# State-space stage of a decoder kernel: other slots for ScalarE's reads, another order of two pieces on TensorE, two decays per unit in SBUF

## The reference, cut to what matters

```python
def _mamba(x, Win, convw, convb, Wx, Wdt, bdt, Alog, Dp, Wout):
    xi, z = jnp.split(x @ Win, 2, axis=-1)               # 256 channels each
    xi = silu(_causal_dwconv(xi, convw, convb))          # 4 taps
    dt_in, Bm, Cm = split(xi @ Wx)                       # 8, 16, 16
    dt = softplus(dt_in @ Wdt + bdt);  A = -exp(Alog)    # A: 256 x 16
    # per channel and state s: h_t = exp(dt_t*A) * h_(t-1) + dt_t*u_t*B_t ;  y_t = sum_s h_t*C_t
    y = _selective_scan(xi, dt, A, Bm, Cm, Dp)           # + u*Dp
    return y * silu(z) @ Wout
# forward and backward, each + x and normed, summed, then relu(. @ W1 + b1) @ W2 + b2, + sum, normed
```

## Time and profile before

| | us |
|---|---|
| median of 3 runs | 5266.18 (5259.53 to 5272.27) |
| the profiled execution | 5254.81 |
| its span in the trace | 5252.9 |
| state-space stage, first scan at 71.0, last at | 2473.7 |
| busy over the span: PE, DVE, ACT, POOL | 4029.3, 4122.6, 2797.7, 2811.0 |
| one scan, one product by C on DVE (mean) | 1.217, 0.661 |
| one decay on ACT, one input on POOL (mean) | 0.688, 1.323 |

### The profile page before, as it was taken

The page is one execution under the profiler, slowest core; times in us unless marked ns, Lnnn a source line. Parts: engine busy times, 40 slices in busy tenths (PEclk is TensorE's granted clock), DMA queues, the critical chain, the costliest instruction groups (busy, mean ns, idle before and its releaser), DMA issues. The chain is left out here.

```text
span 5252.9 us, 104514 instructions
## 1 busy us (share of the span) xinstructions
PE 4029.3 (77%) x29689; PEld 2335.5 (44%) x29692; DVE 4122.6 (78%) x8425; ACT 2797.7 (53%) x6477; POOL 2811.0 (54%) x3454
## 2 busy tenths in 40 slices
PE   5788787878878877877688868886283888789953
PEld 2333333333333333332466646665282666566632
DVE  5998888899888889987588877776145887767778
ACT  4555555555555555554577744444374554444435
POOL 5766666666666666765477742333543222233345
PEclk8988888898888888988799979996695999889965
DMA  2111110111111111100455535555114554365521
GB/s 87 69 39 67 71 71 37 71 71 67 38 71 71 39 69 71 71 35 39 94 108 105 105 78 118 113 116 159 51 53 119 108 108 99 75 129 116 111 56 32
DMA packets 320704, 420.70 MB, mean 80 GB/s; under 512 B 40512, under 2 KB 302224, under 8 KB 309648
## 3 DMA queue, kind: packets, MB, share of 16 engines
q1 hardware_dynamic: 316048, 408.35, 29.9%
q0 software_dynamic: 4352, 8.95, 0.5%
HBM read 307.65 MB, written 109.58 MB: 79 GB/s over the span
## 5 line engine op out<-in xcount | busy, mean ns | idle before, releaser
L1861 PE MATMUL bank<-m_h,ident 128*128 128x512 f32 x2048 | 1241.8, 701 | 423.8 <-DVE m_h L2127 371.7
L2228 POOL TENSOR_TENSOR m_h<-m_dtu,m_Bb 128x512 f32<-128x512 f32 x1024 | 1327.0, 1323 | 336.5 <-PE bank L1861 331.0
L2121 DVE TENSOR_TENSOR_SCAN m_h<-bank,m_h 128x512 f32<-128x512 f32 x1024 | 1246.3, 1217 | 192.8 <-ACT bank L2009 183.8
L2009 ACT ACTIVATE bank<-m_dt,m_A 128x512 f32<-128x512 f32 x1024 | 695.4, 688 | 748.0 <-DVE m_h L2121 662.0
L1861 PEld LDWEIGHTS bank<-m_h,ident 128*128 128x128 f32 x2048 | 390.7, 214 | 1081.4 <-DVE m_h L2127 847.1
L2127 DVE TENSOR_TENSOR m_h<-m_h,bank 128x512 f32<-128x512 f32 x1024 | 676.8, 661 | 6.7 <-PE bank L1854 6.7
L712 DVE TENSOR_REDUCE x_nm<-bank 128x4 f32<-128x308 f32 x512 | 239.3, 474 | 149.9 <-PE bank L370 144.3
L547 ACT ACTIVATE x_sm<-bank,x_nm 128x77 f32<-128x77 f32 x1024 | 318.2, 336 | 60.3 <-DVE x_nm L712 59.9
L537 ACT ACTIVATE f_pT<-bank 128x512 f32<-128x512 f32 x256 | 153.0, 598 | 239.9 <-PE bank L390 238.6
L1805 PE MATMUL bank<-m_xTp,m_wck 128*128 128x512 f32 x512 | 268.7, 630 | 12.1 <-ACT m_xTp L1923 12.1
L537 ACT ACTIVATE a_pT<-bank 128x512 f32<-128x512 f32 x256 | 153.4, 599 | 181.3 <-PE bank L390 180.3
(11 more groups left out here) (425 smaller groups left out, 9876.4 us busy)
## 6 DMA issues: line engine op xcount, KB each, us to landing
m_Bb<-m_B SPq DMA_DIRECT2D x32, 4096.0 KB, 12.2
x_Ks<-x_k_parts SPq DMA_DIRECT2D x64, 231.0 KB
x_q_parts<-x_qp SPq DMA_DIRECT2D x32, 384.0 KB, 3.9
x_Qs<-x_q_parts SPq DMA_DIRECT2D x32, 384.0 KB
f_Ks<-f_k_parts SPq DMA_DIRECT2D x32, 384.0 KB
a_Ks<-a_k_parts SPq DMA_DIRECT2D x32, 384.0 KB
x_xp<-x_stage SPq DMA_DIRECT2D x32, 256.0 KB
x_Qs<-x_q_parts SPq DMA_DIRECT2D x32, 256.0 KB
```

Of the source, the lines that this page charges most:

```text
L1861: pe.matmul(banks[4 + c], ident[:], h[:, k % RING, :], start=(s == 0), stop=(s == NS - 1)).then_inc(s_ya.sem, 1)
L2009: act.activation(decays[k % AHEAD], dt[:, d, c, :], ACT.Exp, scale=A[:, d, c, s:s + 1]).then_inc(s_dA.sem, 1)
L2121: v.tensor_tensor_scan(h[:, k % RING, :], decays[k % AHEAD], h[:, k % RING, :], 0.0, ALU.mult, ALU.add).then_inc(s_h.sem, 1)
L2228: pool.tensor_tensor(h[:, k % RING, :], dtu[:, d, c, :], Bb[:, d, s, :], ALU.mult).then_inc(s_dB.sem, 1)
```

## The change

The two extra decay buffers are in SBUF (`spare_decays`); `decay_buffer` picks them for slots 26 and 27 of d=0 and 25 and 26 of d=1. `last_reader` gives the scan that last read a buffer, in place of the fixed k-2: for a decay in SBUF it lies in the unit before, and for the next decays in the banks four slots back. `exp` is parted into `exp` and `one`. In `PE_AT` of d=1 `xT` comes ahead of `f:0`; `yT`, `m0`, `m1` and (in d=1) `dt0`, `dt1` move one to three slots back. In `ACT_AT` the reads of `f`, `c1`, `dt0`, `yT`, `m0`, `m1`, `o` move back by up to five slots, `dt1` of d=0 moves two slots forward, `log` and `move` move back; in `DVE_AT` `f_stats`, `f_affine`, `e`, `o_stats`, `dtu` of d=1 follow. `POOL_AT` stays.

```diff
--- before.py
+++ after.py
@@ -1541,7 +1541,6 @@
     SL = NS * NC
     RING = 8
     LAG = 2
-    AHEAD = 2
     TURNS = NG // 2
     PADS = CK - 1
     BROW, CROW, XM = 32, 64, 96
@@ -1592,19 +1591,22 @@
 
 
     PE_AT = ({0: ["xT"], 1: ["c0:0"], 2: ["c0:1", "o:0", "c0:2"], 7: ["o:1", "c0:3"], 8: ["o:2"], 10: ["z0"], 11:
-              ["c1:0", "c1:1", "c1:2", "c1:3"], 14: ["z1", "xd:0", "xd:1"], 17: ["dt0"], 18: ["dt1"], 21: ["yT:0"],
-              22: ["yT:1"], 24: ["m0"], 27: ["m1"]},
-             {0: ["f:0", "xT"], 1: ["f:1", "c1:0"], 2: ["c0:0"], 3: ["c1:1", "c1:2"], 6: ["c0:1"], 7: ["c1:3"], 8:
-              ["c0:2"], 9: ["c0:3"], 12: ["z0"], 14: ["z1", "xd:0", "xd:1"], 16: ["dt0"], 17: ["dt1"], 21: ["o:0"],
+              ["c1:0", "c1:1", "c1:2", "c1:3"], 14: ["z1", "xd:0", "xd:1"], 17: ["dt0"], 18: ["dt1"], 22: ["yT:0"],
+              23: ["yT:1"], 27: ["m0"], 28: ["m1"]},
+             {0: ["xT", "f:0"], 1: ["f:1", "c1:0"], 2: ["c0:0"], 3: ["c1:1", "c1:2"], 6: ["c0:1"], 7: ["c1:3"], 8:
+              ["c0:2"], 9: ["c0:3"], 12: ["z0"], 14: ["z1", "xd:0", "xd:1"], 17: ["dt0"], 18: ["dt1"], 21: ["o:0"],
               23: ["o:1", "o:2"]})
-    ACT_AT = ({0: ["xT"], 10: ["c0"], 11: ["o"], 12: ["z0"], 14: ["o_norm", "c1"], 16: ["z1"], 17: ["xd"], 19: ["dt0"], 23: ["dt1", "exp", "yT"], 25: ["log"], 26: ["move"], 27: ["m1"], 29: ["m0"]},
-              {0: ["xT"], 1: ["f"], 6: ["f_norm"], 10: ["c1"], 12: ["c0"], 13: ["f_out"], 14: ["z0"], 16: ["z1", "xd"], 20: ["dt0"], 21: ["dt1"], 22: ["exp"], 24: ["log", "o"], 26: ["move"], 29: ["o_norm"]})
+    ACT_AT = ({0: ["xT"], 10: ["c0"], 11: ["o"], 12: ["z0"], 14: ["o_norm", "c1"], 16: ["z1"], 17: ["xd"], 20: ["dt0"],
+               21: ["dt1"], 22: ["exp"], 23: ["one"], 27: ["log"], 28: ["yT"], 29: ["move"], 30: ["m0"], 31: ["m1"]},
+              {0: ["xT"], 4: ["f"], 9: ["f_norm"], 11: ["c1"], 12: ["c0"], 14: ["z0"], 15: ["f_out"], 16: ["z1"], 17: ["xd"],
+               20: ["dt0"], 21: ["dt1"], 22: ["exp"], 23: ["one"], 26: ["log"], 27: ["o"], 28: ["move"], 31: ["o_norm"]})
     DVE_AT = ({0: ["y"], 11: ["o_stats"], 14: ["z0", "u"], 15: ["z0_read"], 17: ["z1"], 18: ["z1_read"], 22: ["rest"], 23:
                ["e"], 29: ["lo"], 30: ["dtu"]},
-              {2: ["y", "f_stats"], 8: ["f_affine"], 13: ["u", "z0"], 14: ["z0_read"], 15: ["z1"], 16: ["z1_read"], 21: ["rest"],
-               22: ["e"], 25: ["o_stats"], 28: ["dtu"], 29: ["lo"]})
+              {2: ["y"], 5: ["f_stats"], 10: ["f_affine"], 13: ["u", "z0"], 14: ["z0_read"], 15: ["z1"], 16: ["z1_read"],
+               21: ["rest"], 23: ["e"], 27: ["o_stats"], 29: ["lo"], 30: ["dtu"]})
     POOL_AT = ({4: ["gated"], 15: ["o_pow"], 31: ["dt", "far"]},
                {8: ["f_pow"], 13: ["out_pow"], 14: ["gated"], 26: ["dt"], 30: ["o_pow"], 31: ["far"]})
+    IN_SBUF = ((26, 27), (25, 26))
     LAST = ("y", "gated", "o", "o_stats", "o_pow", "o_norm")
 
     def side(at, g, d, k):
@@ -1612,7 +1614,7 @@
         for what in at[d].get(k, []):
             name = what.split(":")[0]
             kind = name if name in PREP else ("o" if name in LAST else ("f" if name[0] == "f" and name != "far" else name))
-            if kind in ("u", "z0_read", "z1_read", "move", "exp", "log", "rest", "lo", "e", "dtu", "dt", "far"):
+            if kind in ("u", "z0_read", "z1_read", "move", "exp", "one", "log", "rest", "lo", "e", "dtu", "dt", "far"):
                 kind = "xT"
             if kind == "out_pow":
                 kind = "f"
@@ -1692,7 +1694,19 @@
         x_g, o_g = [t.rearrange("(g b) t d -> g t b d", b=GB) for t in (x, y)]
         turned_by = (ident, flip)
         convw = Bb[:, 0, 0:4, :].rearrange("p a t -> p (a t)")
-        decays = (banks[0], banks[1])
+        spare = sb("spare_decays", [P, 2, GT])
+
+        def decay_buffer(d, k):
+
+            return spare[:, k % 2, :] if k in IN_SBUF[d] else banks[k % 2]
+
+        def last_reader(d, k):
+
+            back = 2
+            while ((k - back) % SL in IN_SBUF[(d + (k - back) // SL) % 2]) != (k in IN_SBUF[d]):
+                back += 2
+            return k - back
+
         block = st.enter_context(nc.Block())
 
         def schedule(turn):
@@ -1958,6 +1972,7 @@
                 if what == "exp":
                     act.wait_ge(s_ab.sem, s_ab.at(n + 1))
                     act.activation(flat(cc[:]), flat(cc[:]), ACT.Exp, scale=-1.0).then_inc(s_z.sem, 1)
+                if what == "one":
                     act.wait_ge(s_z.sem, s_z.at(n + 1))
                     act.activation(flat(tu[:]), flat(cc[:]), ACT.Identity, bias=one[:]).then_inc(s_w1.sem, 1)
                 if what == "log":
@@ -2005,8 +2020,8 @@
                 s, c = k // NC, k % NC
                 if k == 0:
                     act.wait_ge(s_dt.sem, s_dt.at(n + 1))
-                act.wait_ge(s_h.sem, s_h.at(n, k + 1 - AHEAD))
-                act.activation(decays[k % AHEAD], dt[:, d, c, :], ACT.Exp, scale=A[:, d, c, s:s + 1]).then_inc(s_dA.sem, 1)
+                act.wait_ge(s_h.sem, s_h.at(n, last_reader(d, k) + 1))
+                act.activation(decay_buffer(d, k), dt[:, d, c, :], ACT.Exp, scale=A[:, d, c, s:s + 1]).then_inc(s_dA.sem, 1)
 
             def work(at, what, g, l, d):
 
@@ -2029,7 +2044,7 @@
                 for l in range(2):
                     for d in range(2):
                         unit(2 * i + l, l, d)
-            for what in ("xT", "c1", "c0", "z0", "z1", "xd", "move", "dt0", "dt1", "exp", "log"):
+            for what in ("xT", "c1", "c0", "z0", "z1", "xd", "move", "dt0", "dt1", "exp", "one", "log"):
                 prep(use_first, 0, 0, what)
             schedule(turn)(act)
             for d, names in ((0, ("o", "o_norm", "yT", "m0", "m1")), (1, ("f", "f_norm", "f_out"))):
@@ -2118,7 +2133,7 @@
             def scan(v, n, d, k):
                 v.wait_ge(s_dA.sem, s_dA.at(n, k + 1))
                 v.wait_ge(s_dB.sem, s_dB.at(n, k + 1))
-                v.tensor_tensor_scan(h[:, k % RING, :], decays[k % AHEAD], h[:, k % RING, :], 0.0, ALU.mult, ALU.add).then_inc(s_h.sem, 1)
+                v.tensor_tensor_scan(h[:, k % RING, :], decay_buffer(d, k), h[:, k % RING, :], 0.0, ALU.mult, ALU.add).then_inc(s_h.sem, 1)
 
             def times_C(v, n, k):
                 s = k // NC
```

## The result

The changed kernel takes 5185.08 us (median of 4 runs, 5177.53 to 5197.9) against 5262.85 for the kernel before (4 runs, 5259.41 to 5272.27): a ratio of 0.9852, 95% interval 0.9827 to 0.9877, so 65 to 91 us less. Forecast were 5201, in a range of 5122 to 5240.

What follows compares the result with a forecast made beforehand. DVE, busy 2170.64 of the state-space stage's 2406.00 us, was taken as the bound. Gross gain 165 less 98 and 2 gives 65 us: the profiled 5254.81 becomes 5190, the median 5201; range 5122 to 5240.

Steps and rivals of the forecast that it cites:

- waits for ScalarE: Scans' waits for decays at slots 24 to 28 go; 32 us stay at slot 1 of d=1: 152 us gained.
- `lo`: In d=1, every second unit, it meets GpSimd idle instead of mid-inputs: 0.7 us, where it took 1.75; 10 us gained.
- waits for the spread C: Products on DVE waiting for TensorE's spread C, 6.7 us: half of it goes, 3 us gained.
- scans 25, 26 and input 27 of d=1: SBUF-decay scans meet GpSimd's two `dt` operations, making input 27 late for scan 27: 4.4 us a unit lost.
- scans 26, 27 of d=0: SBUF-decay scans meet GpSimd's input 31 and first `dt`: between 0.7 and 2.7 us, taken as 2.0 a unit lost.
- input 0 of the next unit: `dtu` one to two slots later in d=1 leaves GpSimd's input 0 just in time: 16 x 0.1 = 2 us lost.
- The lock: DVE operations with both inputs in SBUF wait for a running GpSimd operation; two scans a unit now do: 98 us with input 27.
- no lock: Rival: SBUF-decay scans are not held by GpSimd, only input 27 is late; 130 us gained, 5136 us; chance 0.20.
- GpSimd keeps the ports for its whole queue: Rival: waiting scans in slots 25 to 28 are not let in between GpSimd operations; 90 us slower, 5356 us; chance 0.06.
- input 27 is tied to `e`: In d=1, fixed durations from `e` through logarithm and `dt` make input 27 late for scan 27: 2.2 us without port conflicts.
- part 3: TensorE's `xT` ahead of `f:0` at the start of d=1 shortens scan 1's wait: 1.34 us, 1.6 at half clock.
- part 1: Side results read later on ScalarE: the slot 28 wait of d=0 (3.78 us) and the 5 us pile-up before decay 24 go.

Runs made afterwards that it cites:

- Experiment 1: Changed kernel with all decays back in the two PSUM banks, none in SBUF; 5176.79 us, ratio 0.9862.
- experiment 2: Changed kernel with one SBUF decay a unit, at slot 30 where GpSimd is idle, instead of two; 5180.45 us, ratio 0.9844.
- experiment 4: Changed kernel with each of GpSimd's two `dt` operations split into two of 512 columns, in the old place; 5170.34 us, ratio 0.9854.
- Experiment 10: Changed kernel with ScalarE's read of `xT` in slot 2 of both units instead of slot 0; 5165.36 us, ratio 0.9835.
- experiment 8: Kernel before the change, with only TensorE's `xT` put ahead of `f:0` in slot 0 of d=1; 5264.04 us, ratio 1.0005.
- Experiment 7: Changed kernel with TensorE's `f:0` put back ahead of `xT` in slot 0 of d=1; 5190.06 us, ratio 0.9889.
- experiment 3: Changed kernel with GpSimd's `dt` of d=1 moved behind the unit's last input, in slot 31; 5156.16 us, ratio 0.9813.
- experiment 5: Changed kernel, SBUF decays kept, with `dt` of d=1 behind input 31 and every `dt` operation in two halves; 5155.75 us, ratio 0.9792.
- experiment 6: Changed kernel with all decays in the PSUM banks and `dt` of d=1 behind input 31; 5138.29 us, ratio 0.9759.

## Why the prediction was right, and where it was off

Its steps by DVE's own account in the stage, in us (minus is a gain):

| step | forecast | came |
|---|---|---|
| waits for ScalarE, 183.8 to | 32: -152 | 40.1: -143.7 |
| `lo` | -10 | 31.5 to 21.6: -9.9 |
| waits for the spread C | -3 | 6.7 to 9.3: +2.6 |
| scans 25, 26 and input 27 of d=1 | 15 x 4.4 = +66 | 49.3 + 8.8 = +58 |
| scans 26, 27 of d=0 | 16 x 2.0 = +32 | 16 x 2.2 = +35 |
| input 0 of the next unit | +2 | other waits for inputs 5.5 to 4.3: -1.2 |
| `u` (in the range, 16 either way) | 0 | 46.5 to 59.4: +12.9 |
| `rest`, `e` | 0 | +5.8, -1.4 |
| `y` | 0 | 19.9 to 24.6: +4.7 |
| statistics and affine (`o_stats`, `f_affine`) | 0 | 22.5 to 12.9, 27.4 to 20.6: -16.4 |
| sum | -65 | -54, stage -61.9 |

Some 8 us of the stage lie in groups that I did not follow.

*Luck.* That 61.9 came for 65 is in part luck. The rows with a forecast of 0 moved by 41 us, some up and some down, and their sum is only +5.6. And the median fell by 77.8 us, not 65; of the 77.2 us of the profiled executions 15 lie outside the stage, where nothing was changed.

*Gain, right.* The waits at slots 24 to 28 went as a whole, and those at slot 1 stayed. Experiment 1 shows that this did not need the SBUF decays, to which the prediction gave the waits beside the logarithm: without them 24.5 us come back at slots 28 and 29 of d=0 and 70.0 at input 27, and 83.8 us of stretch go.

*The lock, right in mechanism and size.* The walk had scans 25, 26, 27 of d=1 at S+4.55, S+8.2 and S+12.4; they came at S+4.56, S+8.03 and S+11.92. For d=1 the stretches of a full unit are 2.97 - 1.22 and 2.72 - 1.22, and 0.59 for input 27. For d=0 the scans take 1.93 and 2.66 on average, less 1.22 each. Experiments 1, 2 and 4 exclude another cause: without the SBUF decays there is no stretch, without GpSimd there is none, and with halves on GpSimd the longest is 1 us shorter. So "no lock" is out. "GpSimd keeps the ports for its whole queue" is out as well: a waiting scan was let in after one operation, 2.98 us at most.

*Too short: how far input 27 is tied to `e`.* I had a wait of 2.2 us in the case without a lock, with decays made ahead; no run has that case. Experiment 1 shows what else holds the logarithm: decay 26, queued ahead of it, which waits for a bank. There the wait is 5.26 us. The step "input 27 is tied to `e`" should have read "to the logarithm, which waits for `e` or for the decays ahead of it". The forecast itself was not touched by that.

*Mis-sized: what is left at slot 1*, 40.1 us for 32, or 2.67 each for 2.1. I carried over eight short and seven long ones, and that was misread: the kernel before has six short (2.82 to 3.06) and nine long (4.46 to 5.76), which by my own sizes, 1.5 and 2.9, make 35 us. Ten long ones of 3.25 came, by TensorE's clock. Experiment 10 shows what the place is worth once it is cleared: 40.1 us, of which 16.5 come back at `y`.

*`u`, in the range but not in the sum.* 31 operations of 1.50 us became 31 of 1.92, though neither `u` nor GpSimd's list moved. It has two inputs in SBUF. It takes 1.50 us on average in experiment 8, which has part 3 alone, and 1.89 to 1.92 in all variants with part 1, with or without SBUF decays. The trace of the changed kernel settles what it is: all 31 begin inside a GpSimd operation and end 1.08 us after it, as the scans do; before, 17 of 31 did. The statistics and the affine got shorter the same way: 18 of 61 and 7 of 30 of their operations began inside a GpSimd operation before, 9 and none do now. I counted only `lo` of this kind. Why `u` always meets an input now is only argued: DVE without its stalls is nearer to GpSimd in time. The growth of `y` and of the waits for C is not explained.

*Part 3* was costed at 15 x 1.3 to 1.6 us at slot 1. Experiment 7 found 11.9 us there, with other clocks, and no difference in total; alone (experiment 8) it is worth nothing, because the read of `f` then waits in slot 2. That it gave its 20 us in the changed kernel is not shown.

## What to carry to other kernels

A wait that is cleared by moving a reader later in an in-order queue is cheap; look first there, and put a long operation directly behind what it depends on, before buying buffers. An operand moved from PSUM to SBUF makes a DVE operation with two inputs meet GpSimd: price it by the GpSimd operations that it meets in its slots, per unit, and expect GpSimd's queue behind it to be late too. After each cleared wait compare the busy time of unchanged instructions as well as the waits: here 83.8 us of new waiting were recorded as DVE being busy.

## What the runs showed of the hardware

**A stall inside the record.** A scan of 1.22 us is recorded with up to 2.98 us when it waits for GpSimd, with no idle time before it; GpSimd's `dt` goes from 2.35 to 3.14 or 3.27 us in the same way. I had expected the mechanism, but not that each side is let in after exactly one operation of the other: in the changed kernel every held DVE operation, and every held input of GpSimd, ends its own time after the one operation in which it began.

**An operation with one input is held too.** The statistics' `TENSOR_SCALAR`, 128x4 with one input in SBUF, takes 0.17 us alone. When it begins inside a GpSimd operation it ends 0.02 to 0.03 us after that: 9 of 61 in the changed kernel, up to 0.45 us, and 15 of 61 in experiment 3, up to 2.19. The scans with their decay in PSUM have one input in SBUF too, and none of the 960 is held.

**TensorE's clock at the change of units.** In the changed kernel PE stands idle 1.42 and 1.51 us ahead of the last sums before d=1 begins (1.50 at this place before), and then gets half the clock. The stretches around it (us, busy PE, PEld, DVE, ACT, POOL, then PEclk), first of the changed kernel, then at the same place of the one before:

```profile
1016.00:1020.00 4.00, 2.01 (x5) 0.40 (x3) 3.97 (x5) 0.69 (x2) 0.56 (x2) 0.99 0.00 0
1020.00:1024.00 4.00, 3.06 (x8) 2.03 (x9) 2.68 (x4) 0.24 (x1) 4.00 (x4) 0.50 0.00 0
```

```profile
1031.40:1035.40 4.00, 2.00 (x5) 0.39 (x3) 3.98 (x5) 0.69 (x1) 1.46 (x3) 1.00 0.00 0
1035.40:1039.40 4.00, 3.96 (x24) 3.01 (x25) 1.80 (x2) 0.57 (x2) 4.00 (x4) 1.00 0.00 0
```

Both have been busy for half of the time ahead of the change, and one falls to 0.50 of full speed (1.2 GHz) where the other keeps 1.00 (2.4 GHz). In the timeline of the changed kernel the sums and `xT` then take about twice as long, and scan 1 waits 3.25 us instead of 1.48:

```profile
1020.94 2.08 PE L1875 MATMUL bank<-m_h,ident 128*128 128x512 f32 x2 [1.51 <-DVE m_h L2142]
...
1022.80 1.92 PE L1815 MATMUL bank<-ident,m_xg 128*128 128x128 f32 x8
...
1025.97 1.22 DVE L2136 TENSOR_TENSOR_SCAN m_h<-bank,m_h 128x512 f32<-128x512 f32 x1 [3.25 <-ACT bank L2024]
```

By the length of the wait at scan 1, of 15 such places 10 are at half clock in the changed kernel, 9 in the one before, none in experiment 1, 4 in experiment 7. It goes with the two SBUF decays a unit: with them 10, 9, 12 and 9 (the changed kernel, experiments 3, 4 and 5) and 4 (experiment 7), without them, but with part 1, 0, 1 and 0 (experiments 1, 2 and 6). `y` in slot 0 of d=0 waits 0.56 us at full clock and 1.6 to 2.9 at half; there 10 of 15 places are at half clock in the changed kernel, none in experiment 1, 1 in experiments 4 and 7, 6 in experiment 6, so that for this place the buffers are not what counts. It is not one execution's accident: the granted clock of a whole run is 0.868 to 0.871 in the four of the changed kernel and 0.874 to 0.879 in the four of experiment 1. What in a schedule decides it, no run here shows. It makes differences of 10 to 20 us in the waits at slot 1 and at `y` that an edit's own place does not explain.
